# Two stacked low-rank products per tile, eleven gate and up tiles, and new places for sums, loads and roundings in the first network

## The reference, cut to what matters

```python
# D 256, F 688, 8 experts, top 2, rank 8; scale 1/8
scores = sigmoid(x @ W_router);  w = top-2 of (scores + expert_bias), normalised
gate = x @ W_gate + x @ sA_gate @ sB_gate*scale + sum_e w_e * (x @ A_gate[e] @ B_gate[e])*scale
up   = x @ W_up   + x @ sA_up   @ sB_up*scale   + sum_e w_e * (x @ A_up[e]   @ B_up[e])*scale
hidden = silu(gate) * up
out = hidden @ W_down + hidden @ sA_down @ sB_down*scale + sum_e w_e * (hidden @ A_down[e] @ B_down[e])*scale
```

## Time and profile before

| | us |
|---|---|
| median of 3 runs | 1399.97 (1399.4 to 1401.15) |
| the profiled execution | 1409.79 |
| its span | 1408.0 |
| its mean granted clock | 0.984 |
| PE busy | 1350.0 (96%) |
| DVE, ACT, POOL busy | 993.7, 611.3, 566.9 |

### The profile page before, as it was taken

The page is one execution under the profiler, slowest core; times in us unless marked ns, Lnnn a source line. Parts: engine busy times, 40 slices in busy tenths (PEclk is TensorE's granted clock), DMA queues, the critical chain, the costliest instruction groups (busy, mean ns, idle before and its releaser), DMA issues.

```text
span 1408.0 us, 24791 instructions
## 1 busy us (share of the span) xinstructions
PE 1350.0 (96%) x8292; PEld 1108.4 (79%) x8292; DVE 993.7 (71%) x2519; ACT 611.3 (43%) x1497; POOL 566.9 (40%) x466
## 2 busy tenths in 40 slices
PE   8999999999999999899999999999999999985995
PEld 7788888888888888788887888888888888863664
DVE  5788888888888888865454565765765666874226
ACT  4555555555555555642323333433433434441332
POOL 3776656565656565802104232222222212313222
PEclk9999999999999999999999999999999999987998
DMA  6000000000000200120000200200200002777994
GB/s 190 1 12 1 13 0 11 0 11 0 11 0 11 66 0 1 21 70 1 0 1 0 76 8 16 76 9 16 75 8 15 8 9 53 203 260 227 282 266 135
DMA packets 67952, 76.16 MB, mean 54 GB/s; under 512 B 14189, under 2 KB 55173, under 8 KB 67877
## 3 DMA queue, kind: packets, MB, share of 16 engines
q1 hardware_dynamic: 56533, 58.36, 14.3%
q10 hardware_dynamic: 8560, 12.36, 3.0%
q0 software_dynamic: 2784, 4.46, 1.6%
HBM read 66.22 MB, written 8.95 MB: 53 GB/s over the span
## 4 chain that ended last, share of the span: by engine, by line
PE 83%; DVE 6%; ACT 4%; issue 3%; DMA 2%; another core or an unknown queue 1%; POOL 0%; SPq 0%; DVEq 0%; ACTq 0%; POOLq 0%
PE ps L1857 43%; PE ps L2003 9%; PE ps L1958 6%; PE ps L2040 4%; PE ps L1964 2%; PE ps L2225 2%; PE ps L1978 2%; PE ps L1974 2%; PE ps L1975 2%; DMA wo<-in_L_attn_wo_dram 1%; PE ps L2215 1%; PE ps L2452 1%; PE ps L2138 1%; PE ps L2374 1%; PE ps L2139 1%
## 5 line engine op out<-in xcount | busy, mean ns | idle before, releaser
L860 ACT ACTIVATE probs<-ps,nm 128x128 f32<-128x128 f32 (+3 forms) x256 | 135.4, 529 | 198.7 <-DVE nm L1277 198.7
L717 POOL TENSOR_TENSOR qk<-q,ksb 128x512 f32<-128x512 f32 x64 | 85.7, 1340 | 306.2 <-ACT q L978 214.6
L2003 PE MATMUL ps<-kT,qT 128*128 128x128 f32 (+3 forms) x512 | 159.3, 434 | 3.2 <-ACT probs L860 3.2
L1209 DVE TENSOR_TENSOR prod<-ps,rope_sb 128x1024 f32<-128x1024 f32 x128 | 155.5, 1217 | 7.3 <-PE ps L1857 7.3
L557 POOL TENSOR_TENSOR qT<-prod 64x512 f32<-64x512 f32 x64 | 82.0, 1281 | 140.5 <-DVE prod L1209 133.3
L1187 DVE TENSOR_TENSOR pT_low<-ps,pT 128x384 fp32r<-128x384 f32 (+2 forms) x256 | 104.8, 451 | 44.4 <-ACT pT L794 44.4
L1277 DVE CUSTOM_DVE_ANT_0 ps<-ps,causal 128x128 f32<-128x128 f32 (+3 forms) x256 | 122.7, 500 | 3.1 <-PE ps L2003 3.0
L557 POOL TENSOR_TENSOR kT<-prod 64x512 f32<-64x512 f32 x64 | 82.1, 1282 | 70.2 <-DVE prod L1209 64.8
L1857 PEld LDWEIGHTS ps<-kvo,qn 128*128 128x128 f32 x768 | 100.8, 192 | 8.6 <-DVE qn L1187 3.9
L1331 DVE SCALAR_TENSOR_TENSOR acc<-ps,rinv,acc 128x256 f32<-128x256 f32 x256 | 106.0, 476 | 2.1 <-issue 2.1
L794 ACT ACTIVATE pT<-ps 128x384 fp32r<-128x384 f32 (+2 forms) x256 | 84.9, 415 | 51.4 <-PE ps L2040 51.3
(11 more groups left out here) (303 smaller groups left out, 3046.9 us busy)
## 6 DMA issues: line engine op xcount, KB each, us to landing
eg<-in_L_ffn_w_gate_dram SPq DMA_DIRECT2D x16, 704.0 KB
eg<-in_L_ffn_w_up_dram SPq DMA_DIRECT2D x16, 704.0 KB
ed<-in_L_ffn_w_down_dram ACTq DMA_DIRECT2D x10, 640.0 KB
ksb<-ks_dram SPq DMA_DIRECT2D x16, 256.0 KB, 3.3
ed<-in_L_ffn_w_down_dram SPq DMA_DIRECT2D x6, 640.0 KB
rows_dram<-rows ACTq DMA_DIRECT2D x4, 640.0 KB, 7.7
acc<-in_L_attn_x_dram SPq DMA_DIRECT2D x4, 512.0 KB
wq_in<-in_L_attn_wq_dram SPq DMA_DIRECT2D x8, 256.0 KB, 2.9
```

What stands on the lines that cost most here:

```text
L717: nc.gpsimd.tensor_tensor(qk[:], q3[:], ksb[b % 2][:], ALU.mult).then_inc(qk_ready, 1)
L860: nc.scalar.activation(probs[hh][:, off:off + (i + 1) * P], ps[:, BS + i % 2, 0:(i + 1) * P], ACT.Exp, bias=nm[:, hh, i:i + 1], scale=-1.0 ...
L1209: nc.vector.tensor_tensor(prod[parity][w][:], ps[:, BA:BA + 2, :], rope[:, w:w + 1, :].broadcast_to([P, 2, T]), ALU.mult).then_inc(product ...
L2003: pe.matmul(ps[:, bank, 0:(i + 1) * P], qT[:, hh, b, i * P:(i + 1) * P], kT[:, hh, b, 0:(i + 1) * P], start=True, stop=True).then_inc(scor ...
```

## The change

The tiles of the hidden features become five of 128, 128, 128, 128 and 112, and a last one of 64, whose gate and up columns lie side by side in the weights, so that one product of 128 output rows makes both (gate in rows 0 to 63 of a bank, up in rows 64 to 127). For that the up matrix is stored with its last 64 columns first, and 64 zero columns stand between them and the gate columns in the low-rank weights. The three low-rank passes become two: one contracts 128 rows (high weights by the high and the low half of the first 64 ranks), the other 104 (low weights of all 72, and the last 8 ranks' other two products).

```diff
-F0S = [(i * 115, 115) for i in range(4)] + [(460, 114), (574, 114)]
+F0S = [(i * 128, 128) for i in range(4)] + [(512, 112), (624, 64)]
@@ sync: the order of the small loads
-                for w, name in enumerate(("gate", "up")):
-                    sp.dma_start(lb_in[0:R0, w, :], ...); sp.dma_start(lb_in[R0:NL, w, :], ...)
...
+                for w, name in enumerate(("gate", "up")):
+                    for to, lo, hi in ((0, 0, F0),) if w == 0 else ((F0 + size, f, F0), (F0 + 2 * size, 0, f)):
...
+                        sp.dma_start(lb_in[NL:NX, cols], io["L0_ffn_B_" + name][E0 - 1][:, lo:hi]).then_inc(lb_loaded, 16)
@@ gpsimd, ahead of the weight pieces
             pool.wait_ge(roped, 4 * PROJECTIONS)
-            pool.wait_ge(gu_loaded, 32)
+            nc.gpsimd.memset(lb_rest[64:96].bitcast(F32), 0.0).then_inc(rows_zeroed, 1)
+            nc.gpsimd.memset(xaT_rest[64:96].bitcast(F32), 0.0).then_inc(rows_zeroed, 1)
+            pool.wait_ge(rows_zeroed, rows_zeroed_first + 2)
+            nc.gpsimd.memset(lb_in[:, F0:F0 + F0S[-1][1]], 0.0).then_inc(rows_zeroed, 1)
+            pool.wait_ge(rows_zeroed, rows_zeroed_first + 3)
+            pool.wait_ge(gu_loaded, 48)
@@ scalar, last step of the attention, behind the oT_high copy
+                if last and n == STEPS - 1:
+                    act.wait_ge(rows_zeroed, rows_zeroed_first + 3)
+                    act.wait_ge(lb_loaded, 144)
+                    copy(lb_rest[64:NX], lb_in[64:NX]).then_inc(lb_copied, 1)
@@ scalar, xa_halves
-                    copy(xaT[0][:, w, :], ps[0:NL, xa_bank(b) + w, :]).then_inc(xahi_ready, 1)
+                    copy(xaT_wide[0:64, w, :], ps[0:64, xa_bank(b) + w, :])
+                    copy(xaT_rest[0:NX, w, :], ps[0:NX, xa_bank(b) + w, :]).then_inc(xahi_ready, 1)
@@ scalar, behind scores0(0)
+            act.wait_ge(w0_lo, w0_first + 6)
+            copy(lb_wide[64:P], lb_in[0:64])
+            copy(lb_rest[96:NB], lb_in[64:NL])
@@ vector, route0
+                for k in range(2):
+                    nc.vector.tensor_tensor(xa[:, 2 * k:2 * k + 2, :]...[:, :, :, NL:NX], ...)  # 32 elements each
@@ vector, xa_rests
-                    rest(xaT[1][:, w, :], ps[0:NL, xa_bank(b) + w, :], xaT[0][:, w, :]).then_inc(xalo_ready, 1)
+                    rest(xaT_wide[64:P, w, :], ps[0:64, xa_bank(b) + w, :], xaT_rest[0:64, w, :])
+                    rest(xaT_rest[96:NB, w, :], ps[64:NL, xa_bank(b) + w, :], xaT_rest[64:NL, w, :]).then_inc(xalo_ready, 1)
@@ vector, end of ffn0
                     take_weights()
-                    xa_rests(b + 1)
...
                 dve.wait_ge(ffn_added, b * TPB + TPB)
                 if not last:
+                    xa_rests(b + 1)
                     statistics(tiles(b), 2 * b + 3)
@@ tensor
+                if m == FT0 - 1:
+                    for k in range(KD):
+                        mm3(ps[:, m % 2, :], lambda a: gu[a][:, k, f:f + 2 * size], lambda c: x1T[b % 2][c][:, k, :], k == 0, False)
+                    return
...
-                    last = mm3(ps[0:size, 2 * w + m % 2, :], lambda a: lb[a][:, w, f:f + size],
-                               lambda c: xaT[c][:, w, :], False, True)
+                    pe.matmul(ps[0:wide, bank, :], lb_wide[:, at:at + wide], xaT_wide[:, w, :], start=False, stop=False)
+                    last = pe.matmul(ps[0:wide, bank, :], lb_rest[:, at:at + wide], xaT_rest[:, w, :], start=False,
+                                     stop=w == 1 or m < FT0 - 1)
```

More of the change, by code:

```diff
@@ L29 @@
 NA = E0 + 2 * NL
+NX, NB = 80, 104
 FT0 = 6
-F0S = [(i * 115, 115) for i in range(4)] + [(460, 114), (574, 114)]
-M0 = 115
+F0S = [(i * 128, 128) for i in range(4)] + [(512, 112), (624, 64)]
+M0 = 128
+LB = 2 * F0 + F0S[-1][1]
 E1, I1, CAP, TOP1 = 64, 176, 32, 6
@@ L119, in program @@
         oT_low = place("oT_low", 197, [P, T], F32R)
-        gu_in = place("gu_in", 89, [P, KD, 2, F0])
-        lb_in = place("lb_in", 137, [NL, 2, F0])
+        gu_in = place("gu_in", 89, [P, KD, 2 * F0])
+        lb_in = place("lb_in", 137, [NX, LB])
         dn = place("dn", 174, [M0, FT0, D + NL])
@@ L128, in program @@
         ldn = place("ldn", 140, [NL, D])
-        gu = [place(f"gu{h}", 20 + 11 * h, [P, KD, 2, F0], F32R) for h in range(2)]
-        lb = [place(f"lb{h}", 42 + 5.5 * h, [NL, 2, F0], F32R) for h in range(2)]
-        la = [place(f"la{h}", 53 + 1.25 * h, [P, KD, NA], F32R) for h in range(2)]
+        gu = [place(f"gu{h}", 20 + 11 * h, [P, KD, 2 * F0], F32R) for h in range(2)]
+        lb_wide = place("lb_wide", 42, [P, LB], F32R)
+        lb_rest = place("lb_rest", 47.625, [NB, LB], F32R)
+        la = [place(f"la{h}", 53.25 + 1.25 * h, [P, KD, NA], F32R) for h in range(2)]
         x1T = [[place(f"x1T{i}{h}", at + 4 * h, [P, KD, T], F32R) for h in range(2)] for i, at in enumerate((60, 102))]
-        xaT = [place(f"xaT{h}", 56 + 12 * h, [NL, 2, T], F32R) for h in range(2)]
+        xaT_wide = place("xaT_wide", 68, [P, 2, T], F32R)
+        xaT_rest = place("xaT_rest", 56, [NB, 2, T], F32R)
         gated = [place(f"gated{h}", 72 + 2 * h, [M0, T]) for h in range(2)]
@@ L139, in program @@
         haT = place("haT", 88, [NL, T])
-        xa = place("xa", 90, [P, TPB, 2 * NL])
+        xa = place("xa", 90, [P, TPB, 2 * NX])
         ha = place("ha", 92.5, [P, TPB, NL])
@@ L363, in wait_gathered @@
                 engine.wait_ge(gathered[q], 16 * (GROUPS // 4))
-        w0_pieces = [([h[:, k, w, :] for h in gu], gu_in[:, k, w, :]) for w in (1, 0) for k in range(KD)]
+        w0_pieces = [([h[:, k, F0 * w:F0 * w + F0] for h in gu], gu_in[:, k, F0 * w:F0 * w + F0]) for w in (1, 0) for k in range(KD)]
         w0_pieces.insert(2, ([h[:] for h in la], la_in[:]))
-        w0_pieces.append(([h[:] for h in lb], lb_in[:]))
+        w0_pieces.append(([lb_wide[0:NX], lb_rest[0:NL]], lb_in[:]))
         def x1_bank(b):
@@ L939, in dn_halves @@
                     copy(dn_high[1][:, 0:1, :], dn[:, 3:4, :])
-                    copy(dn_high[1][0:114, 1:3, :], dn[0:114, 4:6, :]).then_inc(dn_hi, 1)
+                    copy(dn_high[1][0:112, 1:2, :], dn[0:112, 4:5, :])
+                    copy(dn_high[1][0:64, 2:3, :], dn[0:64, 5:6, :]).then_inc(dn_hi, 1)
             def ffn0(b, last):
@@ L947, in ffn0 @@
                         act.wait_ge(hid_ready, b * FT0 + (m - 1))
-                    nc.scalar.activation(gated[m % 2][0:size, :], ps[0:size, m % 2, :], ACT.Silu).then_inc(gated_ready, 1)
+                    o = gated[m % 2][0:size, :] if m < FT0 - 1 else gated[m % 2][64:64 + size, :]
+                    nc.scalar.activation(o, ps[0:size, m % 2, :], ACT.Silu).then_inc(gated_ready, 1)
                     act.wait_ge(hid_ready, b * FT0 + (m + 1))
@@ L1432, in dn_rest @@
                     rest(dn_low[:, 3:4, :], dn[:, 3:4, :], dn_high[1][:, 0:1, :])
-                    rest(dn_low[0:114, 4:6, :], dn[0:114, 4:6, :], dn_high[1][0:114, 1:3, :]).then_inc(dn_lo, 1)
+                    rest(dn_low[0:112, 4:5, :], dn[0:112, 4:5, :], dn_high[1][0:112, 1:2, :])
+                    rest(dn_low[0:64, 5:6, :], dn[0:64, 5:6, :], dn_high[1][0:64, 2:3, :]).then_inc(dn_lo, 1)
             def ffn0(b, last):
@@ L1440, in ffn0 @@
                         wait_past(dve, down_ready, b * TPB)
-                    nc.vector.tensor_tensor(hidT[0:size, m, :], gated[m % 2][0:size, :], ps[0:size, 2 + m % 2, :],
-                                            ALU.mult).then_inc(hid_ready, 1)
+                    if m < FT0 - 1:
+                        nc.vector.tensor_tensor(hidT[0:size, m, :], gated[m % 2][0:size, :], ps[0:size, 2 + m % 2, :],
+                                                ALU.mult).then_inc(hid_ready, 1)
+                    else:
+                        nc.vector.tensor_tensor(hidT[0:size, m, :], gated[m % 2][64:64 + size, :], ps[64:64 + size, m % 2, :],
+                                                ALU.mult).then_inc(hid_ready, 1)
                     if m:
@@ L2071, in turn_xa @@
                     for i in range(TPB):
-                        last = pe.transpose(ps[0:NL, xa_bank(b) + w, i * P:(i + 1) * P], xa[:, i, w * NL:(w + 1) * NL], ident[:])
+                        last = pe.transpose(ps[0:NX, xa_bank(b) + w, i * P:(i + 1) * P], xa[:, i, w * NX:(w + 1) * NX], ident[:])
                     last.then_inc(xa_turned, 1)
@@ L2113, in ffn0 @@
                         pe.wait_ge(hid_ready, b * FT0 + (m - 1))
-                        for w in range(2):
+                        for w in range(2 if m < FT0 - 1 else 1):
                             base(m, w)
```

46 lines of the change are left out of this document (33 added, 13 removed).

## The result

| | us |
|---|---|
| kernel after, median of 4 runs | 1413.9 (1412.07 to 1414.3) |
| kernel before, the same runs' other side | 1400.56 (1399.4 to 1401.78) |
| ratio | 1.0094, 95% interval 1.0082 to 1.0106 |
| profiled execution after, its span, its clock | 1414.3, 1412.5, 0.983 |

The kernel became slower by 13.3 us, where no measurable change was forecast (1399.3) and even the range ended at 1403.6.

The account below looks back on a forecast made before the run. PE was taken to bound the kernel, with DVE the hidden bound of each image's first quarter. Gains of 5.0 us less 4.35 for the clock left 0.65: 1399.97 to 1399.3, own range 1396.8 to 1402, 8-in-10 range 1393.8 to 1403.6.

Parts of the forecast that it names:

- Regrouped loads, halvings, 128-row tiles.: New tile sizes: element operations keep 512 columns, down products keep 18 matmuls for a token tile; cost nothing.
- the sum: Gains of 2.60 in image 0, 0.52 each in 1 and 2, 1.36 in 3: 5.0, less 4.35 for clock: 0.65 us.
- (d): Low-rank products: two passes over 128 and 104 rows cost as much as three over 72; 1404.2 us, chance 0.05.
- Matmuls removed, and where they lie: Hidden-feature tiles: 18 matmuls fewer an image at 0.231 us; four ahead of hidT's wait worthless in images 1-3, 14 save 3.23.
- What is late next: End of images 0 to 2: PE waits for the next image's turned rows at first_products, losing 0.84 us of 3.23.
- Sums ahead of the rests: DVE's chain to the first silu: four rests instead of two delay statistics by 1.87 us in images 1, 2 and 3.
- rival (b): Chain to the silu not lengthened, because the rests overlap the statistics' waits; 1389.4 us, chance 0.05.
- The wait that grows: Ahead of tile 2, images 1 to 3: PE stands 4.1 us instead of 0.71; clock falls, costing 1.45 each, 4.35 in all.
- Rival (a): The wait ahead of tile 2 is as long, but the clock holds, so all 5.0 us stay: 1395.0, chance 0.20.
- POOL's memsets, `shift1`, ACT's copies: Memsets ahead of the weight pieces, about 2.5 us, just covered before shift1 (0 to 0.3, taken as 0); ACT's copies covered.
- Rival (c): POOL's memsets take 5.0 us, making shift1 and step 6 2.5 late, and the clock falls, 1.5: 1403.3, chance 0.12.
- Image 0: First image: tile 2 starts 0.46 us earlier, less 0.25 for route0, net 0.21; with 2.39 behind the wait, 2.60 gained.

Follow-up runs that it names:

- the runs with 64, 72 and 128 rows: Kernel before with only new tile sizes, last tile 64 rows: 1412.13 us; last tile 72: 1400.64; kernel after, last tile's down products zero-filled to 128: 1400.77.
- the run with filled waits: Kernel after plus 16 unread products of 512 columns in the wait ahead of tile 2, images 1 to 3: 1407.11 us, ratio 1.0049.
- the padded kernel: Kernel after with the last tile's down products contracting 128 rows, 64 of them zeros written once by POOL: 1400.77 us, ratio 0.9999.
- the kernel with all moves: Kernel after, last down products zero-filled to 128 rows, with ACT's x2 copies, POOL's roots, norm2 and the turning moved: 1386.35 us (0.9890); again 1387.39 (0.9914).
- POOL's work apart: Three POOL waits on DVE's counts added to the kernel with all moves: ratio 0.9881; run again, 1383.15 us, ratio 0.9877.

## Why the prediction was wrong

**The step that failed** is "Regrouped loads, halvings, 128-row tiles. Element operations go by columns, which stay 512: nothing. Down products keep 18 matmuls for a token tile." The count is right, and a count was taken for a price. Two rows of the profile of before, of 128 and of 72 rows, both at 0.231 us a matmul, were read as "whatever the rows". They hold for 72; none of the rows read had 64. The trace of before does have one place with 64 rows, two small transposes in the second attention, and the gap stands ahead of them too:

```profile
1188.21 0.20 PEld L2313 LDWEIGHTS ps<-ident,gw_in 64*128 64x128 f32 x2 [0.17 <-issue]
```

The term belongs in the sum with +3.0 us in each of four images, 12.0 in all, and the runs with 64, 72 and 128 rows show it from three sides. No rival had it either: (d) priced the new low-rank passes, which cost what the forecast said.

**Matmuls removed, and where they lie: right.** The passes start every 0.234, the four ahead of the wait only lengthened it.

**What is late next: right.** PE reaches `first_products` 4.05 us behind the turning (679.25 - 675.20), and without a wait it would have been there after 3.18: 0.87 lost, forecast 0.84 (the text waits until 4.02, though its own reading is 3.99). The 0.68 in the row counts only from the modelled end of the matmul ahead.

**Sums ahead of the rests: mechanism right, size too small.** The prediction let each further rest take 0.60, as the second of the pair did. Four take 0.68 to 0.69 each with gaps between, 2.8 us and not 2.48; statistics start at +5.44 (forecast 5.0) and tile 2 at +13.74, 2.32 later than before where 1.87 was forecast. That is 1.4 us over three images. The chain is lengthened all the same, so rival (b) is out.

**The wait that grows: right in length, 4.24 against 4.1; its price too small.** The clock fell in all three images, to a granted 0.50, as forecast. Twelve matmuls took 2.45, 1.56 and 2.45 us more, together with the first one behind them some 6.7 in all, and 6.3 by the run with filled waits; the forecast had 4.35, drawn from the earlier trace rows, where it recovered sooner (0.70 in the mean from 1303 to 1304, within the twelve matmuls; in after's image 1 it is 0.50 up to 666.4, 5.0 us into them). Rival (a) is out.

**POOL's memsets, `shift1`, ACT's copies: right.** The memsets took 1.29, 0.98 and 0.15 us, the root ended at 584.01 and `shift` started at 584.04, 0.02 before its old time; PE's wait there is 1.74. ACT's copy took 1.40 beside the other work of the step. Rival (c) is out.

**Image 0: too small.** Without the changes of rows it would have gained 0.03 + 2.99 = 3.0; forecast 2.60. Tile 2 starts at 614.00 and not 614.76, 0.76 earlier, where 0.21 was forecast.

**The sum again,** from these readings: image 1 is 2.99 for the changes of rows, 2.6 for the clock, 2.32 for the chain, 0.87 for `x1T`, less 3.23 for the matmuls: 5.55 of 5.66. Image 2, with 1.55 for the clock, gives 4.50 of 4.64, image 3, without `x1T`, 4.68 of 4.69. Of what is left in the first two, 0.10 lies in `first_products`: its first down product follows 2.74 us behind its start (681.99 - 679.25) and did so after 2.64 in before.

That the padded kernel lands within 0.1 us of before, and so within 1.5 of the forecast, is partly luck: its chain and its clock (4.61, 5.49 and 4.50 us for the three twelves) cost some 2.5 us more than forecast, and image 0 gained 0.5 more. Its second attention starts at 784.73, 2.2 us later than in before, where the forecast had it 0.65 earlier; where this comes back behind that was not followed up.

## What to carry to other kernels

A new shape on PE needs a row or a run of that shape before it is costed by its neighbours: here a contraction of 64 rows among wider ones costs 0.19 us at each edge, while 72 rows or zeros up to 128 cost nothing. Before an engine's order is changed, ask which instruction in the chain is there only by that order. Without the changes of rows, the removal of 72 matmuls was worth nothing by itself (0.9999); with ACT's copies, `norm2` and the turning moved, and POOL's work kept off the DVE instructions that PE waits for, the same kernel is 1.2% faster than before (0.9877), while the first of these moves alone gave before 0.26%. And a wait of PE is priced with the fall of its clock: here 2.26 us brought 1.6 more, of which the next wait took most back, and 4.24 us brought 1.6 to 2.6.

## What the runs showed of the hardware

- PE is reported busy all through the changes of rows (13.84 of 13.84 us); only the weight loads' idle time, put down to issue, and matmuls of 0.41 and not 0.31 us show them.
- In before the clock was full behind a wait of 2.16 us. Behind one of 2.26 with 24 dense matmuls it fell: they took 7.40 us against 5.81. Behind 4.24 twelve matmuls took 5.49 twice and 4.60 once in one kernel, so the price of one and the same wait varies by 0.9.
- DVE beside POOL: `x1s` 4.59 against 1.38, an addition 3.37 against 1.22, and a pair of `hid_low` 4.77 in the kernel with all moves against 1.35 with POOL's work apart. POOL is held up in turn (`wk_first` 4.51 there against 2.39).
- One and the same kernel took 625.5 and 614.5 us behind the first network in two profiles. The first has a wait of 12.2 us for something outside this core's engines ahead of the same instruction of ACT, which waits 2.9 us for PE in the second. So before two spans are compared, look in each for a wait put down to "remote".
